# Depthwise 3x3 taps of an attention stage: f32 diagonal products on TensorE's column strips, fed by row-shifted copies of v from device memory

## The chip, the cores and the metric

One core of a Trainium2 chip runs the whole kernel. The metric is the device time of the kernel in microseconds (us), as a median over runs. Times inside the run come from one profiled execution.

## What is computed

Four layers run one after the other on an image batch of 8 x 128 channels x 56 x 56. The change lies in the first of them, a window attention with a depthwise convolution ("lepe") on v. Cut to what matters:

```python
# 49 windows of 8 x 8 pixels per image; 8 heads of 16 channels
proj = xw @ W_qkv + b_qkv                      # q, k, v; 128 channels each
logit = einsum('npc,nqc->npq', q_win * SCALE, k_win)   # window means
_, r_idx = top_k(logit, 4)                     # four windows routed to each window
k_sel, v_sel = kv_pix[r_idx]                   # 4 x 64 keys and values
attn = softmax(einsum('bmqc,bmkc->bmqk', q_h * SCALE, k_sel))
o = einsum('bmqk,bmkc->bmqc', attn, v_sel)
lepe = conv_general_dilated(v_img, lepe_w, padding='SAME', feature_group_count=C) + lepe_b   # 3x3, one filter per channel
out = (o + lepe) @ W_o + b_o
```

Group normalisation precedes the layer and the layer's input is added to its output. The layers behind it are a recurrent one, a masked convolution and a pair of convolutions.

## The kernel before

X, the running activation, stays in SBUF with channels on the partitions: 128 x (8 x 3136). The stage loops over the 8 images (`B`). An image has 7 blocks (`NBLK`) of 8 rows (`BLK` = 448 pixels), and each block holds 7 windows of 64 pixels, so there are 49 windows (`P2`).

For each image, TensorE first forms q, k and v of the seven blocks (lines 1739 to 1747). VectorE evacuates k and v, ScalarE evacuates q and a token-major copy of v (`vst`). SyncE stores `vst` to device memory (`v_windows`, lines 1388 and 1390). VectorE writes v twice into zero-bordered images, `vpad` hi and lo (lines 1609 and 1611): the value rounded to the one-pass type fp32r, and the rest. Then come the window sums, the logits product (L1781), top-k on VectorE, and a transfer of the indices to one row of SBUF (`row`, L1400), from which SyncE, ScalarE and GpSimd load the window numbers into registers.

The 49 windows follow, and every engine's order in them is written out by hand. In step w TensorE does the scores of window w (L1791, four heads' pairs on the row strips), the attended product of window w-2 (L1814, 128 x 32 stationary tiles on the four column strips of bank 6), the turn of window w-1 (L1804, eight transposes), and a `fill(w)` with depthwise products and every seventh window an output product (L1774). ScalarE does four exponentials (L1528) and two copies of turned probabilities (L1537). VectorE does four maxima (L1631), two reciprocals, the fourth pair's normalisation (L1696), the evacuation of the attended product (`attended`, L1662 and L1656), and `between(w)`: additions of output blocks to X (L1638), statistics, and the norm of the following image. GpSimd copies keys (L1455) and normalises (L1465). SyncE fetches three of the four value windows of each step (`gather`), in a loop of three steps; ScalarE's queue fetches the fourth (L1367). A gather for w is issued after the attended product of w-3.

The depthwise part is folded into the output product. Tap k has a full 128 x 128 stationary tile, W_o with its rows scaled by the tap's weights, split in hi and lo (`w_tap`, 18 VectorE instructions at the start). A block takes 27 fp32r products, nine taps in three parts, and the output product of the block adds onto them in bank 7. `LEPE_AT` spreads the 27 of blocks 0 to 5 over windows 3 to 8, 11 to 15, 18 to 22, 25 to 29, 33 to 36 and 40 to 43. Block 6 is done ahead of the windows, six products before the logits product and 21 behind it.

A semaphore wait blocks the engine that carries it, and everything behind it in that engine's order.

## Time and profile before

| | |
|---|---|
| median of 3 runs | 3944.39 us (3941.78 to 3946.97) |
| profiled execution | 3944.6 us, its span 3942.8 us |
| TensorE products, share of the span | 3611.9 us, 92% |
| TensorE weight loads | 3103.1 us, 79% |
| VectorE | 2543.2 us, 65% |
| ScalarE | 2168.5 us, 55% |
| GpSimd | 1835.0 us, 47% |
| route transfers (`row`) of images 3, 4 and 5 issued at | 482.97, 697.38, 912.18 us |

The span goes from the first to the last instruction. A product counts as busy while it is in flight, so the row of the weight loads says more on how tightly TensorE issues. In the rows listed below in order of time, the first two numbers are an instruction's start and length in us; those in a row with a count cover all of them, and the bracket is the engine's idle time before it and what ended it. The last row of the table shows the period of one image in the attention stage, some 214 to 215 us; the stage takes the first 1750 us of the span or so.

### The profile page before, as it was taken

How to read it: one execution, taken by the hardware profiler on the slowest of the kernel's cores; microseconds unless marked ns; L12 is line 12 of the kernel's file. 1: busy time of each engine (PE TensorE's matmuls, PEld its weight loads, DVE VectorE, ACT ScalarE, POOL GpSimd, SP SyncE). 2: the span in 40 equal slices, each digit the busy share in tenths (PEclk: the TensorE clock that was granted, in tenths of full speed). 3: DMA queues.
4: the chain of work that ended last, by engine and by line, in shares of the span. 5: the costliest groups of instructions: out<-in, count | busy, mean ns of one | idle time of the engine just before them, and what ended most of it. 6: DMA issues, size and time to landing. Idle time of an engine off the chain costs nothing. (4 is left out here: it accounts for less than half of the span.)

```text
span 3942.8 us, 107339 instructions
## 1 busy us (share of the span) xinstructions
PE 3611.9 (92%) x30684; PEld 3103.1 (79%) x30684; DVE 2543.2 (65%) x6194; ACT 2168.5 (55%) x5969; POOL 1835.0 (47%) x3002
## 2 busy tenths in 40 slices
PE   7989898989989898969999999999999958879998
PEld 4656566666656565659999999999999957769888
DVE  6868687777868686863333333333333289989998
ACT  5868687777868686854443333333333334345554
POOL 2737474655646364730003333333334457756665
PEclk9999999999999999989999999999999979989999
DMA  4111111111111111111110000000002100000000
GB/s 167 39 56 39 56 39 55 39 51 45 40 56 39 55 39 55 40 61 48 52 54 0 0 0 0 0 0 0 0 28 64 48 10 1 1 13 33 33 33 33
DMA packets 170042, 140.43 MB, mean 36 GB/s; under 512 B 31776, under 2 KB 158368, under 8 KB 166688
## 3 DMA queue, kind: packets, MB, share of 16 engines
q1 hardware_dynamic: 138400, 123.78, 9.5%
q10 hardware_dynamic: 31360, 12.87, 1.2%
q8 instruction: 179, 2.93, 0.3%
q14 instruction: 103, 0.84, 0.1%
HBM read 83.32 MB, written 53.22 MB: 35 GB/s over the span
## 5 line engine op out<-in xcount | busy, mean ns | idle before, releaser
L193 PE MATMUL bank<-h,w_hh 128*128 128x128 f32 x8032 | 933.8, 275 | 0.0
L193 PEld LDWEIGHTS bank<-h,w_hh 128*128 128x128 f32 x8032 | 917.0, 192 | 0.0
L1528 ACT ACTIVATE Pr<-bank,nmx 128x256 f32<-128x256 f32 x1568 | 722.5, 473 | 276.2 <-DVE nmx L1631 270.3
L238 ACT ACTIVATE h<-bank,bg 128x128 f32<-128x128 f32 x1008 | 370.2, 367 | 818.3 <-PE bank L193 818.2
L1465 POOL TENSOR_TENSOR Pr<-Pr,rden 128x512 f32<-128x512 f32 (+1 forms) x784 | 659.6, 855 | 168.1 <-DVE rden L1691 137.9
L1631 DVE TENSOR_REDUCE nmx<-bank 128x1 f32<-128x256 f32 x1568 | 554.5, 416 | 155.1 <-PE bank L1791 153.8
L1455 POOL COPY kg<-kT 128x64 f32 x1568 | 300.1, 238 | 594.8 <-DMA row<-ix 296.0
L284 DVE SCALAR_TENSOR_TENSOR inp<-bank,b_in,tz 128x256 f32<-128x256 f32 x196 | 85.8, 479 | 697.2 <-ACT tz L221 697.2
L1537 ACT ACTIVATE PT<-bank 128x512 f32<-128x512 f32 x784 | 428.8, 610 | 21.1 <-PE bank L1804 21.1
L257 POOL CAST h_hi<-h 128x512 fp32r<-128x512 f32 x196 | 119.9, 612 | 685.1 <-ACT h L238 685.1
L1804 PE MATMUL bank<-ident,Pr 128*128 128x128 f32 x3136 | 436.2, 283 | 0.0
L1804 PEld LDWEIGHTS bank<-ident,Pr 128*128 128x128 f32 x3136 | 341.3, 142 | 80.9 <-issue 71.6
L967 POOL TENSOR_TENSOR v_ring<-points,v_ring 128x896 fp32r<-128x896 f32 x128 | 291.5, 2299 | 176.0 <-ACT v_ring L997 176.0
L1814 PE MATMUL bank<-PT,vg 128*32 128x128 f32 x6272 | 264.0, 280 | 97.1 <-ACT PT L1537 92.9
L1791 PE MATMUL bank<-kg,qT 32*128 32x256 f32 x3136 | 340.2, 433 | 13.4 <-ACT Pr L1528 8.8
L1814 PEld LDWEIGHTS bank<-PT,vg 128*32 128x32 f32 x6272 | 162.3, 109 | 239.4 <-issue 149.8
L1528 ACT ACTIVATION_READ_ACCUMULATOR Pr<-bank,nmx 128x1 f32 x1568 | 317.9, 203 | 0.0
L658 PE MATMUL bank<-v_ring,u_hi 128*128 128x392 f32 x768 | 267.5, 348 | 53.5 <-POOL v_ring L967 53.5
L1791 PEld LDWEIGHTS bank<-kg,qT 32*128 32x128 f32 x3136 | 168.7, 186 | 151.2 <-issue 69.2
L260 POOL TENSOR_TENSOR h_lo<-h,h_hi 128x512 fp32r<-128x512 f32 x196 | 251.9, 1285 | 35.2 <-POOL h_hi L257 35.2
L659 PE MATMUL bank<-v_ring,u_hi 128*128 128x392 f32 x768 | 262.8, 342 | 0.0
L660 PE MATMUL bank<-v_ring,u_lo 128*128 128x392 f32 x768 | 261.6, 341 | 0.0
(261 smaller groups left out, 7310.9 us busy)
## 6 DMA issues: line engine op xcount, KB each, us to landing
vg<-v_windows SPq DMA_DIRECT2D x1176, 32.0 KB, 2.0
first_gates<-gate_sums SPq DMA_DIRECT2D x28, 512.0 KB, 2.6
gate_sums<-first_gates SPq DMA_DIRECT2D x28, 512.0 KB, 3.6
X<-in_x SPq DMA_DIRECT2D x8, 1568.0 KB, 17.8
vg<-v_windows ACTq DMA_DIRECT2D x392, 32.0 KB, 2.3
x_backup<-X SPq DMA_DIRECT2D x8, 1568.0 KB, 5.8
out<-X SPq DMA_DIRECT2D x7, 1568.0 KB, 5.2
v_windows<-vst SPq DMA_DIRECT2D x56, 192.0 KB, 2.1
```

Of the source, the lines that this page charges most:

```text
L193: ins = pe.matmul(bank[m][:, tt * COLS:(tt + 1) * COLS], w_hh[:, k, m * 128:(m + 1) * 128], prev[:, k, :], start=False, stop=(k == NH - 1) ...
L238: act.activation(h[:, 2 * q + tt, m, :], bank[m][:, tt * COLS:(tt + 1) * COLS], ACT.Tanh, bias=bg[:, 0, m:m + 1]).then_inc(s_h, 1)
L658: pe.matmul(ps, w[0], x[0], start=first, stop=False)
L967: pool.tensor_tensor(halves(v[:, q % 3, 1], h), halves(pts, h), halves(v[:, q % 3, 0], h).bitcast(F32), ALU.subtract).then_inc(s_lo, 1)
L1455: ins = pool.tensor_copy(kg[:, par, r * W2:(r + 1) * W2], kT[:, bass.ds(i * W2, W2)])
L1465: pool.tensor_tensor(Pr[:, par, pairs, :], Pr[:, par, pairs, :], rden[:, par, pairs].unsqueeze(2).to_broadcast([C, k, KEYS]), ALU.mult)\
L1528: act.activation(Pr[:, par, j, :], bank[j][:, 0:KEYS], ACT.Exp, bias=nmx[:, par, j:j + 1], accum_out=den[:, par, j:j + 1])\
L1537: act.activation(PT[:, par, i * 512:(i + 1) * 512], bank[4 + i][:], ACT.Copy)\
L1631: dve.tensor_reduce(nmx[:, par, j:j + 1], bank[j][:, 0:KEYS], AXX, ALU.max, negate=True)\
L1791: pe.matmul(bank[j][:, 0:KEYS], qT[32 * j:32 * j + 32, w, :], kg[32 * j:32 * j + 32, par, :], start=True, stop=True).then_inc(s_S, 1)
L1804: ins = pe.transpose(bank[4 + j // 2][:, (j % 2 * 2 + c) * C:(j % 2 * 2 + c + 1) * C], Pr[:, par, j, c * C:(c + 1) * C], ident[:])
L1814: ins = pe.matmul(bank[6][32 * j:32 * j + 32, 0:C], vg[:, slot, c, 32 * j:32 * j + 32], PT[:, par, (2 * j + c) * C:(2 * j + c + 1) * C], s ...
```

## The change

The depthwise convolution becomes a computation of its own, in f32, ahead of W_o. v is kept once (`vpad`, f32). Each block of rows is stored to a bordered image in device memory (`v_padded`), and read back as a stack `v_rows`: partitions 0 to 31, 32 to 63 and 64 to 95 hold the same 32 channels shifted by 0, 1 and 2 rows, for four groups of 32 channels, one transfer of 232 KB for each row shift. A stationary tile of 96 x 32, three diagonals of tap weights stacked, then sums the three vertical taps of 32 channels in one product. Four groups go to the four column strips of a bank, and three horizontal shifts accumulate: 12 f32 products of 448 columns for a block in place of 27 fp32r ones. All of a block's 12 stand in three fills, four each.

The result is copied out of PSUM into `lepe`, ordered by window, and added where the attended product is evacuated, so the output product now takes o + lepe. Blocks 0 and 1 are done ahead of the windows (block 0 before the logits product) and copied by ScalarE. Blocks 2 to 6 stand in windows 6 to 8, 13 to 15, 20 to 22, 27 to 29 and 34 to 36 and are copied by VectorE. Output products and additions come one window later. SyncE's loop over the windows is written out, with the stack loads in it (`STACK_AT`). The wait counts of `s_cst`, `s_padz` and `NW` are adapted, and one small constant (`eye`) is loaded.

```diff
+STRIP = 32
+STRIPS = C // STRIP
+STACK = 3 * STRIP
...
+        v_img = nc.dram_tensor("v_padded", [C, H + 2, W + 2], F32, kind="Internal").ap()
...
-            lw = sb("lw", [C, 9])
-            w_tap = [sb(f"w_tap_{k}", [C, 9, C], F32R) for k in ("hi", "lo")]
+            lw = sb("lw", [STACK, 3 * STRIPS])
+            eye = sb("eye", [STACK, STRIP])
+            w_tap = sb("w_tap", [STACK, 3 * STRIPS, STRIP])
...
-            vpad = [sb(f"vpad_{k}", [C, H + 2, W + 2], F32R) for k in ("hi", "lo")]
+            vpad = sb("vpad", [C, H + 2, W + 2])
+            vrow = sb("v_rows", [STACK, 2, STRIPS, ROWS, W + 2])
+            lp = sb("lepe", [C, 2, BLK])
...
-            OUT_LAG, ADD_LAG = 2, 3
+            OUT_LAG, ADD_LAG = 3, 4
             STATS_AT = {13: 0, 15: 1, 20: 2, 22: 3, 27: 4, 29: 5, 30: 6}
-            MEAN_AT, VAR_AT = 32, 39
-
-            def lepe_steps():
-
-                at = {}
-                for b in range(NBLK - 1):
-                    last = (b + 1) * NWIN + OUT_LAG
-                    steps = range(3, last) if b == 0 else range(b * NWIN + ADD_LAG + 1, last)
-                    steps = [w for w in steps if w not in (MEAN_AT, VAR_AT)]
-                    for i, w in enumerate(steps):
-                        at[w] = (b, 27 * i // len(steps), 27 * (i + 1) // len(steps))
-                return at
-
-            LEPE_AT = lepe_steps()
+            MEAN_AT, VAR_AT = 33, 40
+
+            LEPE_AT = {NWIN * (b - 2) + 6 + dx: (b, dx) for b in range(2, NBLK) for dx in range(3)}
+            COPY_AT = {NWIN * (b - 2) + 9: b for b in range(2, NBLK)}
+            STACK_AT = {3: 2, 8: 3, 12: 4, 18: 5, 25: 6}
...
+                    sp.wait_ge(s_padz, BORDERS)
+                    for edge in (0, H + 1):
+                        sp.dma_start(v_img[:, edge], vpad[:, edge, :]).then_inc(s_ve, 16)
+                    sp.wait_ge(s_ve, 32)
+
+                    def rows_stored(n, k):
+
+                        sp.wait_ge(s_vi[k % 2], n * (16 * (4 - k % 2)) + 16 * ((k + 2) // 2) + 16)
+                        passed(sp)
+
+                    def stack(n, b, dy):
+
+                        sp.dma_start(vrow[STRIP * dy:STRIP * dy + STRIP, b % 2].rearrange("p i r c -> p i (r c)"),
+                                     v_img[:, b * ROWS + dy:b * ROWS + dy + ROWS]
+                                     .rearrange("(i p) r c -> p i (r c)", p=STRIP)).then_inc(s_rep[b % 2], 16)
...
+                            if b == 0:
+                                sp.wait_ge(s_lp, n * NBLK + 1)
+                                passed(sp)
+                            sp.wait_ge(s_v, n * NBLK + b + 1)
+                            passed(sp)
+                            rows_stored(n, b - 2)
+                            rows = slice(1 + b * ROWS, 1 + (b + 1) * ROWS)
+                            sp.dma_start(v_img[:, rows], vpad[:, rows, :]).then_inc(s_vi[b % 2], 16)
...
+                            if 2 <= b <= 3:
+                                rows_stored(n, b - 1)
+                                for dy in range(3):
+                                    stack(n, b - 2, dy)
...
-                        with sp.Fori(0, P2 // 3) as k:
-                            for i in range(3):
-                                gather(k * 3 + i, i)
-                        gather(P2 - 1, (P2 - 1) % 3)
+                        for w in range(P2):
+                            for dy in range(3):
+                                if w - dy in STACK_AT:
+                                    b = STACK_AT[w - dy]
+                                    if dy == 0:
+                                        sp.wait_ge(s_lp, n * NBLK + b)
+                                        passed(sp)
+                                    stack(n, b, dy)
+                            gather(w, w % 3)
...
+                        act.wait_ge(s_o, n * P2 + 1)
+                        for b in range(2):
+                            act.wait_ge(s_lp, n * NBLK + b + 2)
+                            act.activation(by_row(lp[:, b, :]), bank[7 - b][:, 0:BLK], ACT.Copy).then_inc(s_le, 1)
...
-                    for k in range(9):
-
-                        dve.tensor_scalar(w_tap[0][:, k, :], w_o[:], lw[:, k:k + 1], None, ALU.mult).then_inc(s_cst, 1)
-                        dve.wait_ge(s_cst, 2 * k + 3)
-                        if k == 0:
-                            dve.tensor_scalar(bq[:], eoq[:], vec[:, 5:6], None, ALU.mult).then_inc(s_bq, 1)
-                        dve.scalar_tensor_tensor(w_tap[1][:, k, :], w_o[:], lw[:, k:k + 1],
-                                                 w_tap[0][:, k, :].bitcast(F32), ALU.mult, ALU.subtract)\
-                            .then_inc(s_cst, 1)
+                    dve.tensor_tensor(w_tap[:], eye[:].unsqueeze(1).to_broadcast([STACK, 3 * STRIPS, STRIP]),
+                                      lw[:].unsqueeze(2).to_broadcast([STACK, 3 * STRIPS, STRIP]), ALU.mult).then_inc(s_cst, 1)
+                    dve.wait_ge(s_cst, 1)
+                    dve.tensor_scalar(bq[:], eoq[:], vec[:, 5:6], None, ALU.mult).then_inc(s_bq, 1)
...
-                            vp = [v[:, 1 + b * ROWS:1 + (b + 1) * ROWS, 1:1 + W] for v in vpad]
-                            vps = bank[4 * par + 2][:, 0:BLK].rearrange("p (r c) -> p r c", c=W)
-                            dve.tensor_scalar(vp[0], vps, vec[:, 2:3], None, ALU.add).then_inc(s_vh, 1)
-                            dve.wait_ge(s_vh, n * NBLK + b + 1)
-                            dve.scalar_tensor_tensor(vp[1], vps, vec[:, 2:3], vp[0].bitcast(F32), ALU.add, ALU.subtract)\
-                                .then_inc(s_v, 1)
+                            dve.tensor_scalar(vpad[:, 1 + b * ROWS:1 + (b + 1) * ROWS, 1:1 + W],
+                                              bank[4 * par + 2][:, 0:BLK].rearrange("p (r c) -> p r c", c=W),
+                                              vec[:, 2:3], None, ALU.add).then_inc(s_v, 1)
...
+                        def copy_lepe(b):
+                            dve.wait_ge(s_lp, n * NBLK + b + 2)
+                            dve.wait_ge(s_o, n * P2 + (b - 1) * NWIN + 1)
+                            dve.tensor_copy(by_row(lp[:, b % 2, :]), bank[7][:, 0:BLK]).then_inc(s_le, 1)
...
-                            dve.tensor_scalar(oh[:], bank[6][:, 0:W2], eo[:, 0:1], None, ALU.mult).then_inc(s_om, 1)
+                            if w % NWIN == 0:
+                                dve.wait_ge(s_le, n * NBLK + w // NWIN + 1)
+                            at = slice(w % NWIN * W2, (w % NWIN + 1) * W2)
+                            dve.scalar_tensor_tensor(oh[:], bank[6][:, 0:W2], eo[:, 0:1], lp[:, w // NWIN % 2, at],
+                                                     ALU.mult, ALU.add).then_inc(s_om, 1)
...
-                        def lepe(b, i0, i1, last):
-
-                            for i in range(i0, i1):
-                                k, part = divmod(i, 3)
-                                dy, dx = divmod(k, 3)
-                                at = (slice(None), slice(b * ROWS + dy, b * ROWS + dy + ROWS), slice(dx, dx + W))
-                                ins = pe.matmul(bank[7][:, 0:BLK], w_tap[part // 2][:, k, :], vpad[part % 2][at],
-                                                start=(i == 0), stop=(last and i == 26))
-                            return ins
+                        def lepe(b, dx, to):
+
+                            if dx == 0:
+                                loads = 4 - b % 2
+                                pe.wait_ge(s_rep[b % 2], (n * loads + b // 2 + 1) * 48)
+                            for i in range(STRIPS):
+                                ins = pe.matmul(to[STRIP * i:STRIP * i + STRIP, 0:BLK], w_tap[:, dx * STRIPS + i, :],
+                                                vrow[:, b % 2, i, :, dx:dx + W], start=(dx == 0), stop=(dx == 2))
+                            if dx == 2:
+                                ins.then_inc(s_lp, 1)
...
+                                pe.wait_ge(s_le, n * NBLK + b + 3)
...
-                                b, i0, i1 = LEPE_AT[w]
-                                if i0 == 0 and b == 0:
-                                    pe.wait_ge(s_la, n + 1)
-                                elif i0 == 0:
-                                    pe.wait_ge(s_ev, n * NBLK + b + 1)
-                                lepe(b, i0, i1, False)
+                                b, dx = LEPE_AT[w]
+                                if b == 2 and dx == 0:
+                                    pe.wait_ge(s_le, n * NBLK + 2)
+                                elif dx == 0:
+                                    pe.wait_ge(s_ev, n * NBLK + b - 1)
+                                lepe(b, dx, bank[7])
...
-                        lepe(NBLK - 1, 0, 6, False)
+                        for dx in range(3):
+                            lepe(0, dx, bank[7])
                         pe.wait_ge(s_k, n * NBLK + NBLK)
                         pe.wait_ge(s_ws, n * 2 + 2)
                         pe.matmul(bank[1][0:P2, 0:P2], qs[:], ks[:], start=True, stop=True).then_inc(s_lg, 1)
-                        lepe(NBLK - 1, 6, 27, True).then_inc(s_lp, 1)
+                        for dx in range(3):
+                            lepe(1, dx, bank[6])
```

## Rows read from the trace of the kernel before

**Rows 1.** Stretches of one image: us, busy time of each engine, granted clock, DMA share, GB/s.

```profile
701.02:872.14 171.12, 159.15 (x1706) 112.38 (x1706) 141.85 (x462) 141.91 (x488) 119.22 (x290) 0.98 0.14 39
663.61:701.02 37.41, 34.03 (x132) 21.46 (x132) 20.73 (x39) 19.28 (x36) 0.77 (x4) 0.91 0.26 87
```

**Rows 2.** Order of time, weight loads: scores of windows 3, 6, 11, 16, 41, 48.

```profile
711.34 0.52 PEld L1791 LDWEIGHTS bank<-kg,qT 32*128 32x128 f32 x8 [0.33 <-issue]
...
722.24 0.31 PEld L1791 LDWEIGHTS bank<-kg,qT 32*128 32x128 f32 x8 [0.32 <-ACT Pr L1528]
...
738.57 0.71 PEld L1791 LDWEIGHTS bank<-kg,qT 32*128 32x128 f32 x8 [0.17 <-ACT Pr L1528]
...
757.11 0.31 PEld L1791 LDWEIGHTS bank<-kg,qT 32*128 32x128 f32 x8 [0.31 <-issue]
...
844.26 0.31 PEld L1791 LDWEIGHTS bank<-kg,qT 32*128 32x128 f32 x8 [0.32 <-issue]
...
867.72 0.67 PEld L1791 LDWEIGHTS bank<-kg,qT 32*128 32x128 f32 x8 [0.17 <-ACT Pr L1528]
```

**Rows 3.** Order of time, VectorE, windows 44 to 47: maxima and one addition.

```profile
856.20 1.42 DVE L1631 TENSOR_REDUCE nmx<-bank 128x1 f32<-128x256 f32 x4 [0.69 <-PE bank L1791]
...
859.24 1.40 DVE L1631 TENSOR_REDUCE nmx<-bank 128x1 f32<-128x256 f32 x4
...
861.43 0.68 DVE L1638 SCALAR_TENSOR_TENSOR X<-bank,cb,X 128x448 f32 x1
...
862.48 1.41 DVE L1631 TENSOR_REDUCE nmx<-bank 128x1 f32<-128x256 f32 x4
...
865.66 1.41 DVE L1631 TENSOR_REDUCE nmx<-bank 128x1 f32<-128x256 f32 x4
```

**Rows 4.** Order of time, weight loads: first of a fill, next scores.

```profile
765.96 0.19 PEld L1765 LDWEIGHTS bank<-vpad_hi,w_tap_hi 128*128 128x128 f32 x1
...
767.20 0.31 PEld L1791 LDWEIGHTS bank<-kg,qT 32*128 32x128 f32 x8 [0.32 <-issue]
```

**Rows 5.** Order of time, two f32 products of 448 columns, next to each other.

```profile
676.68 0.92 PE L1740 MATMUL bank<-PT,w_qkv 128*128 128x448 f32 x2
...
677.44 0.92 PE L1742 MATMUL bank<-PT,w_qkv 128*128 128x448 f32 x2
```

**Rows 6.** Order of time, attended product of a window on the column strips.

```profile
771.52 0.43 PEld L1814 LDWEIGHTS bank<-PT,vg 128*32 128x32 f32 x16 [0.70 <-issue]
771.55 0.67 PE L1814 MATMUL bank<-PT,vg 128*32 128x128 f32 x16 [0.33 <-ACT PT L1537]
```

**Rows 7.** Order of time, from the last projections to the first window.

```profile
694.12 0.48 PE L1765 MATMUL bank<-vpad_hi,w_tap_hi 128*128 128x448 f32 x1 [0.24 <-ACT vst L1499]
...
695.59 0.29 PE L1781 MATMUL bank<-ks,qs 128*49 128x49 f32 x2
...
701.02 0.71 PE L1791 MATMUL bank<-kg,qT 32*128 32x256 f32 x8 [0.54 <-POOL kg L1455]
...
702.21 0.47 ACT L1528 ACTIVATE Pr<-bank,nmx 128x256 f32<-128x256 f32 x1 [8.14 <-DVE nmx L1631]
```

**Rows 8.** Loads of X, and the stores' first waiter on ScalarE.

```profile
L1382 SPq DMA_DIRECT2D X<-in_x x7: 432/655/1279, 6.4 to 10.6; - x7
...
DMA to landing us min/median/max: 6.8/17.8/28.0
...
39.28 0.49 ACT L1497 ACTIVATE vst<-bank 128x384 f32<-128x384 f32 x1 [4.75 <-DMA v_windows<-vst]
```

**Rows 9.** DMA issues of the page: KB each, us to landing.

```profile
gate_sums<-first_gates SPq DMA_DIRECT2D x28, 512.0 KB, 3.6
...
vg<-v_windows ACTq DMA_DIRECT2D x392, 32.0 KB, 2.3
```

**Rows 10.** Stretches at an image's end and ahead of it, granted clock.

```profile
665.00:672.00 7.00, 5.79 (x13) 3.22 (x13) 1.11 (x4) 3.10 (x5) 0.00 (x0) 0.53 0.57 233
...
860.00:868.00 8.00, 7.20 (x91) 5.17 (x86) 7.47 (x25) 7.43 (x29) 5.46 (x13) 1.00 0.14 38
```

More of the change, by code:

```diff
@@ L1237, in program @@
             s_q, s_k, s_v, s_V = sem("q_ready"), sem("k_ready"), sem("v_ready"), sem("vtok_ready")
-            s_vh = sem("v_hi_ready")
+            s_rep = [sem(f"v_rows_stacked{i}") for i in range(2)]
+            s_ve, s_vi = sem("v_edges_stored"), [sem("v_rows_stored_even"), sem("v_rows_stored_odd")]
             s_vst = [sem("v_stored_even"), sem("v_stored_odd")]
@@ L1358, in input_scale, with by_row @@
                 dve.tensor_copy(Bb[:, bass.ds(m, 1)], it).then_inc(s_id, 1)
+            def by_row(t):
+                return t.rearrange("p (w r c) -> p r w c", r=ROWS, c=WIN)
             def following(n):
@@ L1406, in _ @@
                         passed(sp)
+                        rows_stored(n, NBLK - 2)
+                        rows_stored(n, NBLK - 1)
                         sp.wait_ge(s_O, n * P2 + 3)
@@ L1431, in _ @@
                 def _(pool):
-                    for k in range(2):
-                        zero_border(pool, vpad[k][:].unsqueeze(1), s_padz)
-                    for sm in (s_xb, s_V, s_tk, s_kg, s_S, s_O, s_T, s_ev, s_nP, s_ex, s_o, s_Tc, s_mx):
+                    zero_border(pool, vpad[:].unsqueeze(1), s_padz)
+                    for sm in (s_lp, s_xb, s_V, s_tk, s_kg, s_S, s_O, s_T, s_ev, s_nP, s_ex, s_o, s_Tc, s_mx):
                         pool.sem_inc(sm, 1)
@@ L1438, in _ @@
                     pool.sem_inc(s_pV, 2)
+                    for k in range(2):
+                        pool.sem_inc(s_vi[k], 16)
                     pool.sem_inc(s_vst[0], 16)
@@ L1715, in _ @@
                     input_var_tensor(pe, 0)
-                    pe.wait_ge(s_cst, 21)
+                    pe.wait_ge(s_cst, 4)
                     pe.matmul(bank[1][:, 0:1], w_o[:], cb[:, 0:1], start=True, stop=True).then_inc(s_cp, 1)
-                    pe.wait_ge(s_cst, 22)
-                    pe.wait_ge(s_padz, 2 * BORDERS)
+                    pe.wait_ge(s_cst, 5)
+                    pe.wait_ge(s_padz, BORDERS)
                     def image(n, more):
@@ L1811, in attend @@
                             pe.wait_ge(s_o, n * P2 + w + 1)
+                            if isinstance(w, int) and w == 0:
+                                pe.wait_ge(s_le, n * NBLK + 2)
                             for j in range(PAIRS):
@@ L1918 @@
         "ident": np.eye(128, dtype=np.float32),
+        "eye": np.tile(np.eye(32, dtype=np.float32), (3, 1)),
         "group4": (ch[:, None] // GROUP == ch[None, :] // GROUP).astype(np.float32) / np.float32(GROUP),
```

39 lines of the change are left out of this document (16 added, 23 removed).

## The prediction

> **What bounds the kernel now.** I read the table of engines first: no engine is at its limit over the whole run, so the stages have to be read one by one. The change touches only the attention stage, eight images of 214 us each. The table of stretches divides one image [rows 1]: 37 us of projections and routing, then 171 us of attention over 49 windows. In the second part ScalarE and VectorE are both busy for 142 of 171 us, and TensorE's 159 us is mostly matmuls in flight: its weight loads, which mark issue, take 112 us. I then listed the weight loads in order of time and took the start of the scores of each window as the clock of the loop [rows 2]. Windows 11 to 15, which carry 27 depthwise products, take 757.11 - 738.57 = 18.54 us, 3.7 us each. VectorE's own order in windows 44 to 46, which have none, shows the other end [rows 3]: its maxima follow each other at 3.04 us in a window with nothing extra, 3.24 us in one with the 0.68 us addition to X, and 3.18 us in one with statistics; in all three VectorE goes on with almost no gap. So a window without a product takes about 3.02 us, with VectorE as close to being the bound as ScalarE, and depthwise work costs time on top, but not its full price.
>
> **Products in the windows.** Before, the fill of five products runs from 765.96 to the next scores at 767.20 [rows 4]: 1.24 us, of which 0.32 us is idle before the scores, so 0.2 us for a product and 0.2 us of net changeover. A block has 27 products, 27 x 0.207 + 5 x 0.2 = 6.6 us in the five windows 11 to 15. They cost 18.54 - 5 x 3.02 - 0.16 (one window's statistics) = 3.3 us: half of TensorE's time comes out as window time, the other half lies beside ScalarE and VectorE.
>
> After, a fill is four f32 products of 448 columns, one on each column strip. One such product takes 677.44 - 676.68 = 0.76 us [rows 5]. Do strips overlap? The attention product of every window is eight f32 products of 128 columns on the same four strips; in series they would take 8 x 0.76 x 128 / 448 = 1.74 us, and they take 0.43 us of loading and 0.67 us to the end [rows 6]. That is four at a time. So a fill is 0.76 us, with the 0.32 us before the scores 1.1 us, in 15 windows of an image (6 to 8, 13 to 15, 20 to 22, 27 to 29, 34 to 36) in place of 29 windows. By the same half, three fills cost 3 x 1.1 x 0.5 = 1.65 us. The bounds are nothing and the whole 3.3 us; I take the half, since windows 11 to 15 are the nearest case.
>
> The Trainium skill, TensorE: Matmul & The Clock Gate, Part 3, gives a measured speedup of 2.38 for three column strips, so less than full overlap. By it a fill would be about 0.2 us longer and the sum 17 us higher; rows 6 speak for full overlap.
>
> **Additions on VectorE.** Each of five blocks brings a copy of 448 columns out of PSUM into the row-major-by-window tile (windows 9, 16, 23, 30, 37). No such copy is in the trace; the nearest is the addition of 0.68 us over the same columns, which stretches a window by 0.2 us [rows 3]. Bounds: nothing, and 0.68 us. I take 0.2 us, but it falls in a run of copy, output, addition and statistics, so four windows are 3.24 + 3.02 + 3.24 + 3.18 = 12.7 us. The attended half becomes a two-tensor instruction over 64 columns, like the one beside it, and costs nothing new. Seven windows are then 3 x 3.02 + 1.65 + 12.7 = 23.4 us.
>
> **The windows of an image [rows 2].** Windows 3 to 5 take 722.24 - 711.34 = 10.9 us; without fills 9.1, -1.8. Windows 6 to 40 take 122.0 us; five times 23.4 is 117.0, -5.0. Windows 41 to 47 take 23.5 us; without fills 4 x 3.02, then 3.02, 3.24, 3.18: 21.5, -2.0. Together -8.8 us.
>
> **Ahead of the windows.** The logits product waits behind depthwise work: before, six products from 694.12 to the logits at 695.59, 1.47 us [rows 7]; after, twelve f32 ones, 3 x 0.76 + 0.3 = 2.6 us. Everything behind, top-k, the route transfer, key copies and the first scores, is 1.1 us later. The second block of twelve has 5.4 us from logits to scores (695.59 to 701.02) and is hidden, as are the two ScalarE copies of about 0.7 us each in ScalarE's 8.1 us idle. If that cover were gone they would cost 0.7 us each. VectorE loses one of its four passes over each projection block; TensorE is back to back there, so that is worth nothing. SyncE gets one more store and, in two blocks, three loads; at about 0.45 us an issue it has room in a 3.5 us block. An image: -8.8 + 1.1 = -7.7 us; eight: -62 us.
>
> **The loads in the windows.** Three transfers of 232 KB for a block stand ahead of the value gathers on SyncE's queue. A 512 KB load lands in 3.6 us, a gather in 2.3 us [rows 9], so I expect below 3.6 us. SyncE issues the gather for w once window w-3 is attended, some 9 us ahead, and each stack comes several windows ahead of its product: hidden, at 0. The unrolled SyncE loop I put at nothing too.
>
> **First image.** SyncE now waits for two edge stores before its first image, and they queue behind seven loads of X, issued from 6.4 us, that land up to 28 us after issue [rows 8], near 38.6 us. Only then do the v stores go out, two issues and a landing later: ScalarE's wait for the first one, which ends at 39.28 us, would end near 41.8, +2.5 us. The eighteen tap instructions that VectorE loses (some 5 us) lie ahead of this wait, which swallows them.
>
> **Sum.** -62 + 2.5 = -59 us. The profiled execution took 3944.6 us (span 3942.8 and 1.8 around it), 0.2 above the median 3944.39: 3886 us. No change means within 0.2%, or 8 us, about what a measurement of this kernel tells apart.
>
> **Rivals.** (a) The strips don't overlap. The loads of the column strips share their rows. Then a fill is 3.0 + 0.3 us, +2.3 in 15 windows at half to full price (17 to 34 us an image); the first twelve products take 9.1 us (+6.8), and the next twelve outrun the routing by 3.9. Against -7.7 us that is +20 to +37 an image, 4107 to 4243 us. It decides from about 0.7 us more a fill (7.5 x 0.7 in windows, 3 x 0.7 ahead of the logits), that is, when only two strips run at once. Against it: rows 6. 7%. The Trainium skill, same page and part, says loads overlap running matmuls only if their row group differs, which is this rival's rule; rows 6 disagree with it.
>
> (b) Hardly any gain: fills come at full price (+1.65 us in each of five runs, 8 us an image) or the copies do (0.5 x 5 more). For it: VectorE has nearly no gap without products, so it can't use all that TensorE gives back. 3920 to 3952 us, 15%, half of it within the 0.2%.
>
> (c) The fills vanish: three in a row are shorter than five were and ScalarE stays fed. -8 us an image more at most, 3815 to 3850 us, 8%. Against it: VectorE has no gap in rows 3, and windows 11 to 15 took 3.7 us.
>
> (d) Gathers late. ScalarE issues one of the four only a window ahead; if a stack makes it land as late as 512 KB do, 3.6 us after issue, the attention product waits 0.6 us, in 15 windows: +9 us an image, 3958 us. For it: one transfer fills all 16 engines. Against it: 232 KB is half of that. 4%.
>
> (e) TensorE's clock. It falls to 1.2 GHz (0.53 granted over seven us) at an image's end, after idle [rows 10]; without products the last 12 windows have less TensorE work. If they ran at the low level, the weight loads of a window, 112 / 49 = 2.3 us [rows 1], would double: up to 27 us an image, 4100 us. Against it: windows 45 and 46 have none either and hold 1.00. 4%.
>
> **Numbers.** My forecast, 3850 to 3920 us, 62%; (a) 7, (b) 15, (c) 8, (d) 4, (e) 4. Faster: 62 + 8 + 8 = 78%; the same 7%; slower 15%. The range reaches over (b) and half of (c): 3832 to 3945 us.
>
> **What would show it.** In the profile after: the eight weight loads of a fill all started within about 0.4 us, and the next scores some 1.1 us after the first of them (a, if 3 us); windows 41 to 44 at 3.0 us (e, if over 4); the logits product 2.6 us after the first depthwise load; seven windows with a block in 23.4 us (b, if over 24.2); the copy's window at 3.2 us; the attention product never ended by a landing of vg (d); in the first image the vst wait ending near 41.8 us. The forecast is wrong if fills cost more than half of their length, since the sum has 15 of them an image and every 0.1 us in each is 12 us.

## The result, and the profile after

The changed kernel takes 3902.47 us (median of 4 runs, 3898.74 to 3903.0), the kernel before 3945.68 us beside it: 43 us less, a ratio of 0.9891 [0.9879, 0.9903]. The forecast was 3886 us, 59 less. The profiled execution took 3898.7 us, its span is 3897.0 us. Two runs further below, one of the kernel before (8564.16 us) and one of the kernel with the loop written out (5065.94 us), stand far off all others and enter no ratio.

The page's table of engines after: busy us, share, instructions.

```profile
PE 3509.7 (90%) x30516; PEld 2922.8 (75%) x30516; DVE 2500.8 (64%) x6153; ACT 2177.0 (56%) x5985; POOL 1837.3 (47%) x2998
```

TensorE loads weights for 180 us less than before. A quarter of that, 43 us, came out as time.

The first question was whether the strips run together. Weight loads of the fill in window 13 of the fourth image and of the scores behind it, in order of time, then TensorE's products of the same stretch:

```profile
734.69 0.16 PEld L1800 LDWEIGHTS bank<-v_rows,w_tap 96*32 96x32 f32 x8 [0.17 <-issue]
735.58 0.31 PEld L1829 LDWEIGHTS bank<-kg,qT 32*128 32x128 f32 x8 [0.73 <-ACT Pr L1567]
```

```profile
734.69 0.96 PE L1800 MATMUL bank<-v_rows,w_tap 96*32 96x448 f32 x8
735.58 0.71 PE L1829 MATMUL bank<-kg,qT 32*128 32x256 f32 x8
```

An f32 product is two passes, so a fill is eight loads. All eight loads lie within 0.16 us, and the next scores start 0.89 us after the first of them; it is 0.89 us in all fifteen fills of this image. In series four products of 448 columns would take four times the 0.76 us of [rows 5]. A fill takes TensorE 0.89 us, a little less than the 1.1 us of the forecast; a fill of five products before took 1.24 us [rows 4].

The table of stretches gives the windows of the fourth image, from scores to scores: windows 6 to 40, then 41 to 47. First the kernel after, then the kernel before over the same windows (busy time of TensorE, its loads, VectorE, ScalarE, GpSimd).

```profile
708.18:825.90 117.72, 107.68 (x1255) 66.34 (x1254) 103.24 (x340) 101.63 (x351) 85.98 (x210) 1.00 0.24 65
825.90:848.79 22.89, 20.04 (x227) 13.50 (x226) 19.50 (x67) 20.58 (x72) 16.53 (x39) 1.00 0.15 42
```

```profile
722.24:844.26 122.02, 114.78 (x1263) 81.53 (x1262) 103.20 (x338) 102.25 (x352) 86.15 (x212) 1.00 0.14 40
844.26:867.72 23.46, 22.18 (x249) 15.72 (x248) 19.10 (x64) 19.41 (x68) 15.43 (x38) 1.00 0.14 39
```

Windows 6 to 40 are 4.3 us shorter, though TensorE loads for 15.2 us less. Windows 41 to 47 lost all their products, 21 of them, and are only 0.6 us shorter: 22.89 / 7 = 3.27 us each, where the forecast had 21.5 / 7 = 3.08. With windows 3 to 5 (9.34 us, before 10.9) the windows give 6.4 us in this image.

Ahead of the windows, TensorE's products in order of time:

```profile
680.63 2.46 PE L1800 MATMUL bank<-v_rows,w_tap 96*32 96x448 f32 x24 [0.33 <-ACT vst L1538]
683.02 0.29 PE L1818 MATMUL bank<-ks,qs 128*49 128x49 f32 x2
683.25 2.46 PE L1800 MATMUL bank<-v_rows,w_tap 96*32 96x448 f32 x24
688.47 1.23 PE L1829 MATMUL bank<-kg,qT 32*128 32x256 f32 x8 [2.76 <-POOL kg L1494]
```

The first twelve hold the logits product for 2.39 us (before 1.47 [rows 7]). The second twelve lie in the wait for the keys: logits to scores is 5.45 us, before 5.43.

The route transfers are issued at 61.10, 269.08, 477.49, 684.79, 893.23, 1101.86, 1309.72 and 1517.45 us, before at 55.22, 270.25, 482.97, 697.38, 912.18, 1124.99, 1339.36 and 1553.83. The period of an image falls from 214.09 to 208.05 us, the first image becomes 5.9 us longer. ScalarE in the first image, in order of time, its waits for a landing:

```profile
40.56 0.49 ACT L1536 ACTIVATE vst<-bank 128x384 f32<-128x384 f32 x1 [10.60 <-DMA v_windows<-vst]
...
52.28 0.49 ACT L1536 ACTIVATE vst<-bank 128x384 f32<-128x384 f32 x1 [1.82 <-DMA v_windows<-vst]
...
56.14 0.49 ACT L1536 ACTIVATE vst<-bank 128x384 f32<-128x384 f32 x1 [1.99 <-DMA v_windows<-vst]
```

The first wait ends 1.3 us later than in [rows 8], earlier than the 41.8 us forecast; two more stand behind it, which neither the kernel before nor the forecast has. The last load of X landed at 36.47 us, so these two do not wait for it. The table of stretches shows what else differs there. First the kernel after, then before:

```profile
41.00:44.00 3.00, 2.09 (x3) 1.18 (x4) 0.62 (x1) 3.00 (x8) 0.00 (x0) 0.50 0.70 226
44.00:50.00 6.00, 6.00 (x20) 3.27 (x19) 2.59 (x5) 3.54 (x8) 0.00 (x0) 0.83 0.96 233
```

```profile
41.00:44.00 3.00, 3.00 (x14) 1.78 (x12) 1.69 (x4) 3.00 (x7) 0.00 (x0) 1.00 0.40 120
44.00:50.00 6.00, 6.00 (x23) 3.37 (x22) 4.30 (x7) 4.73 (x10) 0.00 (x0) 1.00 0.27 76
```

The DMA share is 0.96 where it was 0.27, and the granted clock is 0.50 where it was 1.00. TensorE's weight loads of the same image, the starts of blocks 4 and 5 and of the first depthwise product:

```profile
41.91 0.50 PEld L1774 LDWEIGHTS bank<-PT,w_qkv 128*128 128x128 f32 x2 [7.86 <-ACT PT L1554]
...
47.43 0.30 PEld L1774 LDWEIGHTS bank<-PT,w_qkv 128*128 128x128 f32 x2 [0.17 <-issue]
...
56.92 0.16 PEld L1800 LDWEIGHTS bank<-v_rows,w_tap 96*32 96x32 f32 x8 [2.01 <-issue]
```

Block 4 starts 1.3 us later than before (40.63 us there). It takes 5.52 us in place of 3.48, behind 7.86 us of idle TensorE (2.02 before): 2.0 us. The first depthwise product waits 1.7 us longer behind the last `vst`, and the logits product is held 0.9 us longer. These four are the 5.9 us.

From the page, transfers: KB each, us to landing. The stacks land in 3.3 us. ScalarE's gathers land in 2.2 us (2.3 before [rows 9]), SyncE's in 2.1 (2.0 before).

```profile
v_rows<-v_padded SPq DMA_DIRECT2D x168, 232.0 KB, 3.3
...
v_padded<-vpad SPq DMA_DIRECT2D x56, 232.0 KB, 2.3
...
vg<-v_windows ACTq DMA_DIRECT2D x392, 32.0 KB, 2.2
```

### The profile page after: what moved, and what is told of

Read it like the earlier page. It is cut to its first block and busy times, and to the rows that moved or that the text cites. A ratio compares the mean times of both kernels' runs of the same rounds, so it can differ in the third digit from the quotient of the medians.

```text
span 3897.0 us, 106851 instructions
## 1 busy us (share of the span) xinstructions
PE 3509.7 (90%) x30516; PEld 2922.8 (75%) x30516; DVE 2500.8 (64%) x6153; ACT 2177.0 (56%) x5985; POOL 1837.3 (47%) x2998
## 3 DMA queue, kind: packets, MB, share of 16 engines
q14 instruction: 163, 1.34, 0.1%
## 5 line engine op out<-in xcount | busy, mean ns | idle before, releaser
L196 PE MATMUL bank<-h,w_hh 128*128 128x128 f32 x8032 | 933.8, 275 | 0.0
L196 PEld LDWEIGHTS bank<-h,w_hh 128*128 128x128 f32 x8032 | 917.1, 192 | 0.0
L1829 PE MATMUL bank<-kg,qT 32*128 32x256 f32 x3136 | 410.3, 440 | 31.1 <-POOL kg L1494 22.3
L1829 PEld LDWEIGHTS bank<-kg,qT 32*128 32x128 f32 x3136 | 216.0, 189 | 225.5 <-ACT Pr L1567 155.8
```

What stands on the lines that cost most here:

```text
L196: ins = pe.matmul(bank[m][:, tt * COLS:(tt + 1) * COLS], w_hh[:, k, m * 128:(m + 1) * 128], prev[:, k, :], start=False, stop=(k == NH - 1) ...
L1829: pe.matmul(bank[j][:, 0:KEYS], qT[32 * j:32 * j + 32, w, :], kg[32 * j:32 * j + 32, par, :], start=True, stop=True).then_inc(s_S, 1)
```

## The experiments

Ratios are to the kernel before, run on the same chip; the changed kernel is at 0.9891. Times of an image and of windows are from the profiled execution, those of windows from its fourth image.

**No products in the windows.** The depthwise part of blocks 2 to 6 is not computed, but for one small product at the end of each.

```diff
+if b >= 2 and dx < 2:
+    return
-for i in range(STRIPS):
+for i in range(STRIPS if b < 2 else 1):
+    n_r = ROWS if b < 2 else 1
...
```

> The changed kernel with the twelve products of blocks 2 to 6 cut to one small product each (one strip, one row), so the depthwise part of these blocks is not computed. Theory of the prediction: three fills cost 1.65 us, 8.3 us an image, 66 us in all, so about 3836 us. Rival: windows without products settle at 3.25 us when there are many in a row, not at 3.02 us, and the fills lie almost whole beside ScalarE and VectorE. Then 2 to 3 us an image, 16 to 24 us in all, so about 3882 us, and windows 6 to 40 take about 115 us against 117.7.

3872.67 us, ratio 0.9825 [0.9809, 0.9842], 204.69 us an image. Windows 6 to 40 take 113.28 us, 3.24 us each, so seven windows without products, with a block's copy, addition and statistics in them, take 22.66 us. The table of stretches shows windows 41 to 47 unchanged, 3.27 us each:

```profile
812.59:835.49 22.90, 20.04 (x228) 13.49 (x227) 19.52 (x68) 20.61 (x72) 16.57 (x39) 1.00 0.16 42
```

Two terms of the forecast are thereby measured. Fifteen fills cost 117.72 - 113.28 = 4.44 us of window time, 0.89 us for three where the forecast had 1.65. Seven windows without them take 22.66 us, where the forecast had 23.4 - 1.65 = 21.8: 3.24 us each, not 3.11. The products before cost 122.02 - 113.28 = 8.7 us; the trace counts 128 of them there, so 1.84 us for a block's 27 (forecast 3.3). Some of the 4.44 is given back: the image is only 3.36 us shorter. Over the images, 0.4 us of it lie between the first projection and the logits and 0.4 in windows 0 to 2; why was not looked into.

**Four products on one strip.** Windows only; blocks 2 to 6 come out summed over channel groups.

```diff
-to[STRIP * i:STRIP * i + STRIP, 0:BLK]
+to[STRIP * j:STRIP * j + STRIP, 0:BLK]     # j = i if b < 2 else 0
...
```

> The changed kernel with the four products of each fill in the windows all put on the first column strip, so they can't overlap; the blocks 2 to 6 of the depthwise part come out wrong, blocks 0 and 1 stay as they are. If the strips overlap four deep in the changed kernel, a fill grows from 0.9 to about 3.1 us: at half price +17 us an image, at full price +34, so 4040 to 4170 us. Rival: the strips were not overlapping much anyway, or the windows have slack for a longer fill: under 3950 us.

4150.33 us, ratio 1.0529 [1.0511, 1.0546], 239.96 us an image, 31.9 more. Weight loads of one window in order of time:

```profile
1047.98 0.14 PEld L1801 LDWEIGHTS bank<-v_rows,w_tap 96*32 96x32 f32 x2 [0.17 <-issue]
1048.38 0.11 PEld L1801 LDWEIGHTS bank<-v_rows,w_tap 96*32 96x32 f32 x1 [0.27 <-issue]
...
1050.26 0.11 PEld L1801 LDWEIGHTS bank<-v_rows,w_tap 96*32 96x32 f32 x1 [0.27 <-issue]
1051.10 0.31 PEld L1831 LDWEIGHTS bank<-kg,qT 32*128 32x128 f32 x8 [0.73 <-issue]
```

On one strip a pass follows the other after 0.38 us, and a fill is 3.12 us. This is rival (a) made real, and the changed kernel does not do it. It also shows the slope: 15 x (3.12 - 0.89) = 33.5 us more of TensorE came out as 31.9 us an image, nearly at full price, while the last 15 x 0.89 = 13.4 us cost 3.36 us, a quarter (4.44 us, a third, in the windows alone).

**No copies on VectorE.** Each copy of 448 columns becomes one of 1 column, so the depthwise part is not carried over.

```diff
-dve.tensor_copy(by_row(lp[:, b % 2, :]), bank[7][:, 0:BLK])
+dve.tensor_copy(lp[:, b % 2, 0:1], bank[7][:, 0:1])
```

> The changed kernel with VectorE's five copies of the depthwise result per image cut to one column each, so blocks 2 to 6 of it are not added. Theory of the prediction: 0.2 us a copy, 1 us an image, 8 us in all, about 3894 us. Rival: VectorE is the bound there and each copy costs its whole 0.61 us, 24 us in all, about 3878 us.

3903.53 us, ratio 0.9903 [0.9887, 0.992], 208.45 us an image. In the changed kernel the copy takes 0.61 us of VectorE. Without the five, windows 6 to 40 are 0.1 us shorter in the mean over the first seven images (117.44 for 117.57 us): a copy costs some 0.03 us, not 0.2.

**Small stacks.** The loads in the windows bring one row of one group (7 KB in place of 232).

```diff
-stack(n, b, dy)
+sp.dma_start(vrow[STRIP * dy:STRIP * dy + STRIP, b % 2, 0, 0, :], v_img[0:STRIP, b * ROWS + dy])
```

> The changed kernel with the fifteen stack loads in the windows of an image cut from 232 KB to 7 KB each, so blocks 2 to 6 of the depthwise part use stale rows. Theory of the prediction: the loads are hidden, so 3902 us, within 4 us. Rival: they delay the value gathers, above all ScalarE's, and the windows with them lose up to 0.6 us: 9 us an image, down to 3830 us.

3900.77 us, ratio 0.9896 [0.988, 0.9913]; windows 6 to 40 take 117.73 us, as in the changed kernel (117.72). The loads are hidden, and rival (d) is out. The profiled execution, at 208.92 us an image, is the slowest of four (3910.93 us), with its extra time ahead of the windows.

**Edge stores first.** The two edge stores are issued ahead of the seven loads of X.

```diff
 sp.wait_ge(s_padz, BORDERS)
 for edge in (0, H + 1):
     sp.dma_start(v_img[:, edge], vpad[:, edge, :]).then_inc(s_ve, 16)
+for n in range(1, B):
+    sp.dma_start(X[:, n * HW:(n + 1) * HW], x_in[n]).then_inc(s_ldx[1], 16)
 sp.wait_ge(s_ve, 32)
```

> The changed kernel with the two edge stores issued ahead of the seven loads of X instead of behind them. If SyncE's wait for the edges is what made the first image later (route transfer at 61.1 us against 55.2), the v stores go out from about 24 us and land with the end of the loads as before the change: the route transfer at about 56 us, 4 to 5 us off the time, 3897 us on the scale of the changed kernel's 3902. Rival: the edges are not it, the larger volume of stores and stacks behind them is; then no more than 1.5 us.

3898.9 us, ratio 0.9883 [0.9865, 0.9901]. As a whole time this can't be told from the changed kernel, since the intervals overlap. In the trace the first route transfer goes out at 58.39 us, 2.7 earlier; ScalarE's first long wait ends at 38.72 us:

```profile
38.72 0.49 ACT L1536 ACTIVATE vst<-bank 128x384 f32<-128x384 f32 x1 [8.87 <-DMA v_windows<-vst]
```

The two later waits for a landing are gone. So the edge stores were 2.7 of the 5.9 us, and 0.9 are the logits product. What stays is the clock: TensorE is still idle for 6.14 us ahead of block 4, has a granted clock of 0.50 from 41 to 44 us, and takes 6.22 us for the block, 2.7 more than the 3.48 before. Block 4 starts 0.6 us earlier than in the kernel before, which gives that much back.

**Logits product first.** It goes ahead of block 0's twelve.

```diff
+pe.wait_ge(s_k, n * NBLK + NBLK)
+pe.wait_ge(s_ws, n * 2 + 2)
+pe.matmul(bank[1][0:P2, 0:P2], qs[:], ks[:], start=True, stop=True).then_inc(s_lg, 1)
 for dx in range(3):
     lepe(0, dx, bank[7])
```

> The changed kernel with the twelve products of block 0 put behind the logits product, so all 24 stand behind it. If the routing waits only for the logits, it starts 2.1 us earlier in each image, and the 24 products (4.9 us) just fit into the 5.4 us from logits to scores: 17 us off, 3885 us. Rival: ScalarE's two copies and the 24 products end after the keys are there and hold up the first scores and exponentials, half or less of it: 3894 us or more.

3890.73 us (3884.55 to 3895.28), ratio 0.9858 [0.9841, 0.9876]. But the period of the profiled execution, the slowest of the four, is 207.85 us, 0.2 less and not 2.1. The last experiment shows most of the reason.

**SyncE's loop written out, alone.** The kernel before, with nothing else changed.

```diff
-with sp.Fori(0, P2 // 3) as k:
-    for i in range(3):
-        gather(k * 3 + i, i)
-gather(P2 - 1, (P2 - 1) % 3)
+for w in range(P2):
+    gather(w, w % 3)
```

> The kernel of before with SyncE's loop over the windows written out and nothing else. Theory of the prediction: nothing, within 3 us of before. Rival: the longer code is fetched late and delays gathers: several us slower. A gain would mean that part of the change's effect came from the loop.

3943.45 us, ratio 0.9998 [0.9987, 1.0008]. Nothing, as forecast.

**X one image ahead.** The seven loads at the start are gone; each image's load of 1568 KB is issued in window 6 of the image before.

```diff
+if w == 6:
+    with sp.If(n < B - 1):
+        sp.dma_start(X[:, bass.ds(following(n) * HW, HW)], x_in[bass.ds(following(n), 1)]...)
...
```

> The changed kernel with the loads of X for images 1 to 7 taken out of the start and issued one image ahead, behind the gather for window 6. If the seven loads are what ScalarE's wait of 10.6 us in the first image stands behind, that wait goes: the route transfer of the first image at 48 to 50 us instead of 61.1, 11 to 13 us off, about 3890 us. A load takes some 5 us of all DMA engines in the windows; if that delays gathers or stacks, up to 3 us in each of seven images come back: 3911 us.

3917.18 us, ratio 0.9939 [0.9914, 0.9963], slower than the changed kernel. The first route transfer goes out at 51.11 us, 10 us earlier, but the period is 212.18 us, 4.1 more. The scores of windows 8 and 9 stand at 718.32 and 724.96 us, 6.6 us apart (3.7 in the changed kernel): gathers behind the load land late. The attended product between them, in order of time:

```profile
721.05 0.65 PEld L1857 LDWEIGHTS bank<-PT,vg 128*32 128x32 f32 x16 [2.41 <-DMA vg<-v_windows]
```

The first image's stores do compete with the loads of X; moving those into the windows costs more.

**What sets a bare window?** Three kernels on top of the first experiment, each with one engine relieved. ScalarE's copies of the turned probabilities are cut to half (the other columns keep what was written there once at the start), VectorE's maxima to half of the keys, GpSimd's normalisation to a quarter of the columns.

```diff
-act.activation(PT[:, par, i * 512:(i + 1) * 512], bank[4 + i][:], ACT.Copy)
+act.activation(PT[:, par, i * 512:i * 512 + 256], bank[4 + i][:, 0:256], ACT.Copy)
...
-dve.tensor_reduce(nmx[:, par, j:j + 1], bank[j][:, 0:KEYS], AXX, ALU.max, negate=True)
+dve.tensor_reduce(nmx[:, par, j:j + 1], bank[j][:, 0:KEYS // 2], AXX, ALU.max, negate=True)
...
-pool.tensor_tensor(Pr[:, par, pairs, :], Pr[:, par, pairs, :], ...to_broadcast([C, k, KEYS]), ALU.mult)
+pool.tensor_tensor(Pr[:, par, pairs, 0:kk], Pr[:, par, pairs, 0:kk], ...to_broadcast([C, k, kk]), ALU.mult)   # kk = KEYS // 4
```

> This kernel has no products in windows 6 to 36, as the run with one small product in their place, and ScalarE's two copies of turned probabilities in each window are cut from 512 to 256 columns (the other columns keep what was there, so the attended values are not those of the reference). It asks what sets the 3.24 us of a window without products. The two copies take 2 x 0.61 us; I estimate 2 x 0.38 at half the columns, from 0.47 us for an exponential of 256 columns and 0.61 us for a copy of 512. Theory S (ScalarE sets the window; it is busy for 26.9 of every 29 exponentials' stretch, 90% of windows 41 to 47): 0.4 us less a window, 47 windows, 8 images: 3872 - 150 = 3720 us, window at 2.85 us. Theory V (VectorE sets it): the copies have slack, at most 0.1 us a window, 3835 to 3872 us. Theory R (a ring over all engines, copies on it because the attended product waits for them): between, some 0.2 us a window, 3800 us. My choice: S.

> No products in windows 6 to 36, and VectorE's four maxima of each window read 128 of 256 columns (the maximum is then over half of the keys, which shifts the exponentials by a factor that the normalisation takes out). A maximum takes 0.41 us; at half the columns I estimate 0.27 us, from 0.28 us for a VectorE instruction over 64 columns and 0.41 over 256. VectorE loses 0.5 us a window. Theory V (VectorE sets the window): 0.4 to 0.5 us less, 3872 - 170 = 3700 us, window at 2.8 us. Theory S (ScalarE sets it): the exponentials start earlier after the scores but ScalarE's own work of a window stays at about 3.0 us, so at most 0.15 us less, 3815 to 3872 us. Theory R (ring): about 0.25 us a window, 3780 us. My choice: S.

> No products in windows 6 to 36, and GpSimd normalises 64 of the 256 columns of its three head pairs (the rest of the probabilities stays unnormalised). Its two instructions of a window take 1.04 and 0.67 us; I estimate 0.35 us each. GpSimd loses 1 us a window, and the turn, which waits for it, could start that much earlier. Theory S or V (an engine sets the window): GpSimd is off the path, 0 to 0.1 us a window, 3835 to 3872 us. Theory R (a ring of waits over the engines with GpSimd on it): 0.3 us or more a window, below 3760 us. My choice: 3850 us, since some windows of 3.6 us wait for GpSimd.

The whole times of the first and third, 22468 and 22506 us, say nothing here: their values send the recurrent layer into its second, far longer form, which a flag decides (its products L196 number 102112, not 8032). The attention stage lies ahead of it and can be read: 199.66, 202.03 and 204.52 us an image, against 204.69. The second kernel takes 3856.06 us, ratio 0.9783 [0.9767, 0.9799]. Windows 6 to 40 take 3.16, 3.19 and 3.24 us each. So 0.42 us less of ScalarE a window gives 0.08, 0.53 us less of VectorE gives 0.05, and 0.95 us less of GpSimd gives nothing. Stretches of 110 us within those windows, ScalarE's case, then VectorE's (columns as above):

```profile
691.68:801.68 110.00, 108.35 (x1141) 73.62 (x1141) 101.58 (x341) 85.94 (x348) 85.63 (x211) 1.00 0.25 68
```

```profile
706.60:816.60 110.00, 95.94 (x1126) 65.77 (x1118) 82.45 (x336) 100.78 (x348) 85.14 (x209) 1.00 0.23 63
```

With ScalarE relieved VectorE is busy for 101.6 of 110 us; with VectorE relieved ScalarE is, for 100.8. In the kernel without products it is 99.7 and 99.0. The groups of instructions over the same stretches say the same. ScalarE's exponentials and VectorE's maxima in the first kernel, then VectorE's reciprocals and ScalarE's exponentials in the second, with the idle time ahead of them and what ended it:

```profile
L1571 ACT ACTIVATE Pr<-bank,nmx 128x256 f32<-128x256 f32 x140 | 64.4, 472 | 24.1 <-DVE nmx L1670 24.1
...
L1670 DVE TENSOR_REDUCE nmx<-bank 128x1 f32<-128x256 f32 x140 | 49.2, 412 | 0.1
```

```profile
L1726 DVE RECIPROCAL rden<-den 128x2 f32<-128x2 f32 x35 | 5.8, 166 | 20.5 <-ACT Pr L1567 20.5
...
L1567 ACT ACTIVATE Pr<-bank,nmx 128x256 f32<-128x256 f32 x140 | 64.4, 472 | 9.0 <-DVE nmx L1666 8.6
```

In the kernel without products ScalarE waits 10.4 us for VectorE's maxima, and VectorE's reciprocals 0.9 us for ScalarE. In the first of the three ScalarE waits 24.1 us for the maxima, with hardly a gap ahead of them on VectorE; in the second VectorE's reciprocals wait 20.5 us for ScalarE's exponentials. What one engine is relieved of, it spends waiting for the other. My choice of ScalarE alone failed: each of the two has about 2.9 us of work a window, and relieving one alone gives under 0.1 us. That they bind together is read from these waits; a kernel with both relieved was not run. It matters because in the second kernel ScalarE still waits 8.6 us for maxima although VectorE is often idle, so part of a window is handing over between the two.

**Both orders together.** The edge stores first and the logits product first; nothing is left out.

> The changed kernel with both orders exchanged: SyncE's two edge stores ahead of the seven loads of X, and the logits product ahead of block 0's twelve depthwise products; it computes the same as the reference. The first alone came out at 0.9883 and the second at 0.9858 of the kernel before, the changed kernel at 0.9891. In the trace of the second, the logits product waits 1.16 us for VectorE's sum over windows, so it is only 0.45 us an image earlier, not 2.1, and its first windows give back 0.2 of it: 8 x 0.25 = 2 us in all. Theory 1 (the two gains are those that the traces show, about 2.7 us in the first image and 2 us over the eight): 3902 - 5 = 3897 us, ratio 0.988. Theory 2 (the second order is worth the 0.3% that its run showed, and the first adds): 3888 us, ratio 0.985. My choice: theory 1, 3895 us.

3884.68 us (3882.4 to 3886.5), ratio 0.9851 [0.9835, 0.9868]: the lowest median of the versions that leave nothing out, some 0.4% below the changed kernel, though not told apart from the logits product first alone (0.9858 [0.9841, 0.9876]). The first route transfer goes out at 56.63 us, and the period is 206.38 us. My choice, theory 1 with 3895 us, missed; theory 2 was right on the time. Weight loads in order of time, the first two of seven blocks of projections and the logits, in this kernel and then in that with the logits product first alone:

```profile
646.45 0.50 PEld L1774 LDWEIGHTS bank<-PT,w_qkv 128*128 128x128 f32 x2 [3.60 <-ACT PT L1554]
...
651.54 0.30 PEld L1774 LDWEIGHTS bank<-PT,w_qkv 128*128 128x128 f32 x2 [0.17 <-issue]
...
673.62 0.17 PEld L1816 LDWEIGHTS bank<-ks,qs 128*49 128x49 f32 x2 [0.66 <-DVE ks L1650]
```

```profile
650.62 0.50 PEld L1774 LDWEIGHTS bank<-PT,w_qkv 128*128 128x128 f32 x2 [3.57 <-ACT PT L1554]
...
657.04 0.30 PEld L1774 LDWEIGHTS bank<-PT,w_qkv 128*128 128x128 f32 x2 [0.17 <-issue]
...
679.61 0.17 PEld L1816 LDWEIGHTS bank<-ks,qs 128*49 128x49 f32 x2 [1.16 <-DVE ks L1650]
```

The first block takes 5.09 us in the one and 6.42 in the other; every later block 3.48 us in both. Over the seven images after the first, block to logits is 29.71 us in the changed kernel, 28.72 with the logits first, 27.80 with both. Without block 0 (means 5.12, 6.18 and 5.56 us) it is 24.6, 22.5 and 22.2: the new order gives its 2.1 to 2.4 us, and block 0, at its varying clock, took up to 1.1 of it back. With the logits first alone, windows 0 to 2 also took 10.5 us in place of 10.0, and in one image logits to scores was 1.1 us longer; no run separates why.

## Why the forecast came out as it did

The direction and the main mechanism were right: strips overlap fully, the windows shrink, the front and the first image cost a little. The size was off by 16 us, 43 us where 59 were forecast. Term by term, an image; measured are means over seven images, the first seven for windows and the last seven for what lies ahead of them:

| term | forecast | measured |
|---|---|---|
| windows 0 to 2 | 0 | -0.1 |
| windows 3 to 5 | -1.8 | -1.5 |
| windows 6 to 40 | -5.0 | -4.6 |
| windows 41 to 47 | -2.0 | -0.6 |
| logits product held | +1.1 | +0.9 |
| last `vst` of the image late | 0 | +0.4 |
| block 0 | 0 | -0.9 |
| last scores to the next image's block 0 | 0 | +0.2 |
| period | -7.7 | -6.0 |
| first image, once | +2.5, +1.1 of the front | +5.9 |

**The step that failed in size: "a window without a product takes about 3.02 us".** It was read from three spacings of VectorE's maxima in windows 44 to 46 [rows 3], only one of them of a window with nothing extra. Those are a short stretch behind windows with products. The spacing of windows is uneven (2.3 to 4.4 us in the changed kernel's fourth image), so three neighbours are no mean; a stretch of 35 without products, extras included, takes 3.24 us each, where the forecast's sum comes to 3.11. In windows 41 to 47 this is the whole error: 3.27 us each and not 3.08, 1.4 us an image, 11 us in all.

**"By the same half"** was wrong too. The price of the old block was computed as what 18.54 us leave above 5 x 3.02, and came out at 3.3 us; the measured 1.84 us is 28% of the 6.6 us of TensorE, not a half. Three fills cost 0.89 us, a third of their 2.7 us. In windows 6 to 40 the base too low and the products too dear cancel: 22.66 + 0.89 = 23.55 us for seven windows, forecast 23.4. Rival (c) put the products at nothing, which was too low, on the same wrong base; rival (b)'s reason, that VectorE has nearly no gap, was the truer account of why so little came out, though its full prices were not what happened.

**The copies** cost next to nothing, some 0.03 us and not 0.2: the kernel without them is as fast. The 12.7 us of four windows carried that 0.2 on a base that was too low.

**Ahead of the windows** the logits product is held 0.9 us longer (forecast 1.1). Averaged over seven images, block 0's end to the logits takes 24.6 us where it took 23.2, +1.4 with those 0.9 in it. Nearly all of the rest is a term that the forecast put at nothing, SyncE's new stores and loads among the stores of `vst`. The last `vst` of an image waits for the landing of an earlier store, in the third image the longest. First the kernel after, then before, in order of time:

```profile
472.54 0.49 ACT L1536 ACTIVATE vst<-bank 128x384 f32<-128x384 f32 x1 [2.26 <-DMA v_windows<-vst]
```

```profile
479.03 0.49 ACT L1497 ACTIVATE vst<-bank 128x384 f32<-128x384 f32 x1 [1.27 <-PE bank L1747]
```

That is 1.0 us later behind its block, and the depthwise products behind it start 1.1 us later; over seven images it is 0.4. The last scores of an image to its successor's first projection take 13.1 us where they took 12.9. Block 0 takes 5.12 us in place of 6.00, which returns 0.9. These sum to +0.7 us, and the windows to -6.7. The cover for the second twelve products held: logits to scores is the same 5.4 us.

**First image.** The step "+2.5" had the mechanism (edge stores behind X loads hold the v stores), and the kernel with the edge stores first shows it with 2.7 us; ScalarE's first wait itself ended only 1.3 us later. Two things were left out. With the new stores and stack loads in the queue the later stores land late: the DMA share is 0.96 there, and the last wait for a landing costs 1.7 us. The kernel without the loads of X keeps one such wait, 1.34 us at 46.15 us. And the five us that VectorE loses at the start are not simply swallowed: TensorE starts earlier, sits idle for 7.86 us in place of 2.02, and comes back at a granted clock of 0.50, which costs 2.0 us in block 4. The kernel without the loads of X has a granted clock of 1.00 from 24 to 50 us, and its first image is 10 us shorter.

The Trainium skill, TensorE: Matmul & The Clock Gate, Part 3, would have loads overlap a running matmul only across row groups, and gives 2.38 for three column strips. The runs contradict the first: the loads of four strips that share rows 0 to 95 lie within 0.16 us, and the same four products take 0.89 us on four strips and 3.12 us on one, 3.5 times less. Three strips were not run, so the 2.38 stands untested; these four show no loss by it.

In the trace the scores of the last window start at 1677.38 us where they started at 1719.68, 42.3 us earlier; the two profiled spans differ by 45.8. The 3.5 us between lie behind the stage, in code that did not change. 2.0 of them fall in the products of the masked convolution, 255.8 us in place of 257.8; with both orders these take 257.4 us, with the same code, so this part differs from run to run.

## What to carry over

The price of taking work off an engine is a slope, not a share. Here the first 33 us of fills an image came out at 95%, the last 13 at 25%, where ScalarE and VectorE set the pace; at which length of a fill the price changes was not measured. Measure the bare loop over many steps before pricing what is added to it, and measure both bounds with one kernel each. Here a new store at the start of a queue was better ahead of the bulk loads, and a product that a long chain waits for ahead of products that only a copy waits for; the two together were worth another 0.4%.

## What the runs showed of the hardware

Four column strips run four f32 products at once: eight loads in 0.16 us, and a step of 0.38 us for four passes, which is the step of one pass when all are on one strip. Weight loads ahead of the logits product, in order of time:

```profile
681.40 0.13 PEld L1800 LDWEIGHTS bank<-v_rows,w_tap 96*32 96x32 f32 x4 [0.24 <-issue]
681.78 0.13 PEld L1800 LDWEIGHTS bank<-v_rows,w_tap 96*32 96x32 f32 x4 [0.24 <-issue]
```

The clock's rise at an image's start comes at different moments. Around the first projections after, the table of stretches grants 0.57 and then 1.00:

```profile
651.00:658.00 7.00, 4.50 (x11) 2.40 (x11) 1.98 (x5) 4.03 (x5) 0.00 (x0) 0.57 0.57 232
658.00:665.00 7.00, 7.00 (x31) 4.19 (x30) 4.92 (x9) 5.15 (x10) 0.00 (x0) 1.00 0.32 104
```

That is 1.2 GHz going to 2.4 GHz after the idle time ahead of an image's block 0. Block 0 took 4.9 to 5.3 us in the seven images of the changed kernel, 5.2 to 6.5 before, 5.7 to 6.4 with the logits first, and with both orders 5.1 and 6.1 in turn from image to image. So block 0 moves by over 1 us with no change in its work. What sets the moment was not tested. The runs of one kernel may spread by it: with the logits first they take 3884.55 to 3895.28 us, and the mean granted clock falls from 0.971 in the fastest to 0.968 in the slowest.
